# Gated attention: transposes ahead of sums in each matrix-engine slot, and sums emptied behind the low halves

## The reference, cut to what matters

```python
qn = layernorm(x, ln_q_g, ln_q_b)
q = qn @ Wq * scale
k, v = jnp.split(media @ Wkv, 2, axis=-1)      # 16 heads of 64
sim = jnp.einsum('bhid,bhjd->bhij', q, k)
sim = jnp.where(media_mask[:, None, None, :], sim, neg_inf)
attn = jax.nn.softmax(sim, axis=-1)
out = jnp.einsum('bhij,bhjd->bhid', attn, v)
x = x + jnp.tanh(attn_gate) * (out.reshape(...) @ Wo)
h = layernorm(x, ln_ff_g, ln_ff_b)
x = x + jnp.tanh(ff_gate) * (jax.nn.gelu(h @ W1, approximate=False) @ W2)
```

## Time and profile before

| | us |
|---|---|
| median of 3 runs | 2543.61 |
| lowest and highest run | 2537.76 and 2545.34 |
| profiled execution | 2532.09 |
| its span | 2530.3 |

### The profile page before, as it was taken

One profiled execution on the slowest core, in us unless ns is written; L12 is line 12 of the kernel. 1 busy time (PEld: TensorE's weight loads), 2 busy tenths in 40 slices (PEclk: granted clock), 3 DMA queues, 4 the chain that ended last, 5 costly groups with the idle time before them and its releaser, 6 DMA issues.

```text
span 2530.3 us, 40523 instructions
## 1 busy us (share of the span) xinstructions
PE 2384.6 (94%) x15802; PEld 1893.7 (75%) x15802; DVE 1542.7 (61%) x4193; ACT 1259.6 (50%) x2132; POOL 583.9 (23%) x666
## 2 busy tenths in 40 slices
PE   7778999999999999789999999899999999999998
PEld 4646999999999765456666666455799999999975
DVE  3247777777777426566666666312777777777730
ACT  2135555555555223267777777211555555555521
POOL 0014344444342004200000000000434444434200
PEclk9889999999999999899999999999999999999999
DMA  8710111112110200010000000310011111211010
GB/s 276 207 43 19 44 40 56 44 41 56 41 44 13 85 19 1 13 37 26 25 26 26 25 14 1 119 34 1 19 43 40 56 44 41 56 40 44 13 51 15
DMA packets 36092, 116.18 MB, mean 46 GB/s; under 512 B 4598, under 2 KB 18526, under 8 KB 35534
## 3 DMA queue, kind: packets, MB, share of 16 engines
q1 hardware_dynamic: 33438, 101.30, 13.3%
q10 hardware_dynamic: 2464, 12.29, 1.9%
HBM read 112.66 MB, written 0.92 MB: 45 GB/s over the span
## 4 chain that ended last, share of the span: by engine, by line
PE 85%; DVE 9%; ACT 3%; DMA 1%; issue 1%; POOL 0%; ACTq 0%; SPq 0%; DVEq 0%; POOLq 0%
PE bank L868 19%; PE bank L855 17%; PE bank L880 11%; DVE n_scores L1631 5%; PE bank L1512 4%; PE bank L1499 4%; PE bank L1524 3%; PE bank L1740 3%; PE bank L1090 2%; PE bank L1073 2%; PE bank L691 2%; PE bank L1081 2%; PE bank L1750 2%; PE bank L512 2%; PE bank L1485 1%; PE bank L368 1%
## 5 line engine op out<-in xcount | busy, mean ns | idle before, releaser
L929 ACT CAST p_T_high<-bank 125x512 fp32r<-125x512 f32 x672 | 350.9, 595 | 515.5 <-PE bank L880 515.5
L1002 DVE TENSOR_TENSOR p_T_low<-bank,p_T_high 125x512 fp32r<-125x512 f32 x672 | 422.7, 685 | 258.2 <-ACT p_T_high L929 258.0
L968 DVE CUSTOM_DVE_ANT_0 scores<-bank,mask 128x500 f32<-128x500 f32 x672 | 418.2, 672 | 0.4 <-PE bank L855 0.4
L939 ACT ACTIVATE scores<-scores,row_max 128x1500 f32<-128x1500 f32 x224 | 353.5, 1578 | 9.8 <-DVE row_max L973 9.8
L868 PE MATMUL bank<-p_T_high,keys_nat_high 125*128 125x256 f32 (+1 forms) x1152 | 346.2, 301 | 1.7 <-ACT inverse L936 1.7
L868 PE MATMUL bank<-p_T_high,keys_nat_low 125*128 125x256 f32 (+1 forms) x1152 | 346.1, 300 | 0.0
L868 PE MATMUL bank<-p_T_low,keys_nat_high 125*128 125x256 f32 (+1 forms) x1152 | 345.9, 300 | 0.0
L880 PE MATMUL bank<-ident,scores 128*125 128x128 f32 x2688 | 332.0, 273 | 2.4 <-ACT scores L939 2.4
L880 PEld LDWEIGHTS bank<-ident,scores 128*125 128x125 f32 x2688 | 319.4, 188 | 5.7 <-ACT scores L939 5.7
L1631 DVE CUSTOM_DVE_ANT_0 n_scores<-bank,n_zeros 112x500 f32<-112x500 f32 x384 | 237.5, 675 | 126.9 <-PE bank L1499 126.9
L855 PE MATMUL bank<-keys_T_high,q_stage_high 128*128 128x500 f32 x672 | 281.1, 418 | 10.5 <-DVE q_stage_low L945 6.9
(11 more groups left out here) (197 smaller groups left out, 3234.0 us busy)
## 6 DMA issues: line engine op xcount, KB each, us to landing
ctx_T<-in_ctxT SPq DMA_DIRECT2D x32, 750.0 KB, 4.3
ctx_nat<-in_ctx SPq DMA_DIRECT2D x32, 672.0 KB
q_and_o<-in_ctxT SPq DMA_DIRECT2D x16, 750.0 KB, 9.8
n_ctx_T<-in_ctxT SPq DMA_DIRECT2D x16, 750.0 KB, 4.3
q_and_o<-in_ctx ACTq DMA_DIRECT2D x16, 672.0 KB
mask_bytes<-in_mask SPq DMA_DIRECT2D x32, 187.5 KB, 5.3
weights<-in_L_W SPq DMA_DIRECT2D x4, 1024.0 KB, 9.6
ctx_nat<-in_ctx SPq DMA_DIRECT2D x32, 78.0 KB
```

Source lines behind the costliest of these rows:

```text
L929: e.copy(PTs[0][g % 2][0:KP, 4 * c:4 * c + 4, lo:lo + 128], psum[3 + c][0:KP, :].rearrange("p (k r) -> p k r", k=4)).then_inc(s_eh, 1)
L939: e.activation(SB[s % 2], SB[s % 2], ACT.Exp, bias=mx[:, s % 4, 3:4], accum_out=mx[:, s % 4, 4:5]).then_inc(s_ex, 1)
L968: e.tensor_tensor_reduce(out=SB[u % 2][:, c * CHK:(c + 1) * CHK], in0=psum[c][:, 0:CHK], in1=mb[:, c * CHK:(c + 1) * CHK], scale=1.0, scal ...
L1002: e.tensor_tensor(low, psum[3 + c][0:KP, :].rearrange("p (k r) -> p k r", k=4), high.bitcast(F32), ALU.subtract).then_inc(s_el, 1)
```

## The change

In PE's slot the transposes and the spread of unit s-1 move ahead of the sums; the slot is scores, transposes, spread, sums. In DVE's slot o_out moves behind the three low copies. No instruction is added or removed, and every wait keeps its place ahead of its instruction.

```diff
@@ pe_cross
             for s in range(U + 4):
                 if s < U:
                     scores(s)
-                for g, part, of in work_of(s):
-                    sums(g, part, of)
                 if 1 <= s <= U:
                     transposes(s - 1)
                     if units_of(group_of(s - 1))[-1] == s - 1:
                         spread(group_of(s - 1))
+                for g, part, of in work_of(s):
+                    sums(g, part, of)
@@ dve_cross
                     e.reciprocal(mx[:, u % 4, 5:6], mx[:, u % 4, 4:5]).then_inc(s_rc, 1)
-                for g, part, of in work_of(s):
-                    if part == of - 1:
-                        o_out(g)
                 if 0 <= u < U:
                     g = group_of(u)
                     lo = column(u)
...
                         e.tensor_tensor(low, psum[3 + c][0:KP, :].rearrange("p (k r) -> p k r", k=4),
                                         high.bitcast(F32), ALU.subtract).then_inc(s_el, 1)
+                for g, part, of in work_of(s):
+                    if part == of - 1:
+                        o_out(g)
```

## The result

| | before | after |
|---|---|---|
| median of the runs, us | 2544.48 (4 runs) | 2641.41 (4 runs) |
| lowest and highest, us | 2537.76 and 2546.4 | 2640.32 and 2647.06 |
| profiled execution, us | 2532.09 | 2640.32 |
| its span, us | 2530.3 | 2638.5 |
| ratio, 95% interval | | 1.039 (1.0366 to 1.0415) |

The change makes the kernel 3.9% slower, 96.9 us between the medians. 2647 us was forecast. The ratios of all runs leave out the one disturbed execution, 4013 us among the ten of the kernel with DVE's order alone.

A forecast was written before the change was run, and what follows sets the result against it. PE's instruction stream was taken as the bound. Stalls of 52 us in each gated-attention stage, 104 in both, less 0.5 at their ends, added 103.5 to 2543.6 us: 2647 us, 4.1% slower, range 2610 to 2685.

The forecast's parts named there:

- The bound: Gated-attention stages: PE's own instruction stream bounds them, with almost no idle time a new order could win back.
- The new wait and its slots: In slots 3 and 5 of seven, ACT's high copy waits for sums now behind the transposes, 31 times a stage.
- The size of the conflict stall: PE's transposes wait for Exp behind ACT's waiting copy: 1.23 us plus 0.11 for load, 1.34 us each.
- The load ahead: Twelve transposes that waited for Exp take 1.58 us against 1.47, their weights not loaded ahead: 0.11 us more.
- The second stall: Slot 4's spread waits for DVE's late reciprocal after slot 3's stall: 0.7 us with load, 15 times a stage.
- The sum: Both stages: 41.5 and 10.5 us make 52 in each, 104 in both; less 0.5 at the ends, 103.5 us.
- The prediction's own 0.5: Net gain at starts and ends of stages: 0.83 us of idle covered at the end, about 0.4 lost at the start.
- The 75 us: Changed profile: transposes wait for Exp about 31 times in each stage, near 1.2 us each, 75 us in all.
- The first rival's break point: Not slower, 5 in 100: the copy's delay stays under slack if less than some 0.9 us of sums follow the transposes.
- the slack of 1.62 us: From first copy to next slot's first transpose, 4.77 us, against a copy, Exp and read-out chain of 3.15 us.
- Clock and seams: Within the larger-wait rival, over 2672 us, 10 in 100: seams cost 18 us more, a 0.94 clock up to 80.

The follow-up runs named there:

- both repairs: Changed kernel with ACT's Exp ahead of the three high copies in slots 3 and 5 of seven, and DVE's reciprocal ahead of the maxima: 2543.4 us, ratio 1.0007.

## Why the prediction was right, and where it wasn't

- **The bound** (PE without gaps, nothing to win back): right. The two kernels of these runs that have no new wait in their repeating slots, DVE's order alone and the one with both repairs, give 1.0014 and 1.0007.
- **The new wait and its slots**: right. ACT waited for the sums 62 times, in slots 3 and 5 of seven, and Exp behind it in ACT's queue was shown to be the cause by taking it out of that queue.
- **The size of the conflict stall**: 1.23 us and 0.11 for the load were forecast. The same two distances in the kernel with both repairs give what a slot takes without a stall, 5.46 and 5.50 in the rows shown, so that 6.77 and 6.80 hold stalls of 1.31 and 1.30. The load is 0.11 as forecast (5.59 from 668.57 to 674.16, against 5.48 there, from 683.69 to 689.17). The copy started 3.63 us behind its transposes instead of 3.54, since the first sums matmul now carries the exposed load (it starts 0.26 us ahead of the second, the others 0.17 to 0.19), which the sum had placed at the scores. So 1.42 and not 1.34 us: 62 times 0.08 is some 5 us too little.
- **The load ahead**: the waiting blocks took 1.57 and 1.58 us, the others 1.47, as forecast. The Trainium skill ("TensorE: Matmul & The Clock Gate", Part 2, step 1) has weight loads pulled ahead of matmuls in flight. The rows don't contradict it, as the prediction had it: in the blocks that waited no matmul was left in flight, and there the 0.11 us stands.
- **The second stall**: the mechanism was right (two edits removed it, one enlarged it), the size too large. 0.7 us was forecast. The distance is 6.28 us, against 5.82 in the two kernels that have the conflict stall but not this one: 0.46. The reciprocal ended almost where it was reckoned, 10.70 us behind the start of slot 3's scores instead of 10.75, but only the second transpose of the spread needs it: the first turned unit 2's reciprocal ahead of time (656.90), and no further load shows. 30 times 0.24 is 7 us too much.
- **The sum**: 104 us less 0.5 was forecast, 100.5 lie in the stages, and the medians differ by 96.9. Two mis-sized terms of opposite sign, 5 us and 7 us, nearly cancel, and that is luck. With the measured sizes, 62 times 1.42 and 30 times 0.46, the sum is 102 us, and the starts and ends of the stages with the seams gave back 1 net. (The prediction's own 0.5 for them is a slip: 0.83 gained and 0.4 lost in each of two stages make 0.9.) The remaining 3.6 us between stages and medians is less than the 5.6 us by which an untouched stretch differed. The 75 us that the prediction wanted to see as PE's wait for Exp came out as 74.8 by luck too: 62 stalls are shown with 1.14 us each, some 71 us, and ten short waits at the starts and ends of the stages make up the rest.
- **The first rival's break point**: wrong, though the rival did not come true. "Less than about 0.9 us of sums left behind the transposes" set the sums' end against a fixed place of the next transposes, but that place moves with the sums. With 0.5 to 0.7 us left, the ratio was still 1.0396. The step that failed is the slack of 1.62 us: it was counted from a copy that does not wait.
- **Clock and seams**: neither took part. PE's granted clock stayed at 1.00 in both stages. PE was busy 639 of 685 us in the first, a larger share than the 626 of 682 that was forecast, since busy time grew with the waits, as estimated behind the page above:

```profile
200.00:885.00 685.00, 639.11 (x4158) 578.19 (x4159) 472.86 (x1289) 370.08 (x620) 251.70 (x290) 1.00 0.13 37
1830.00:2520.00 690.00, 643.76 (x4172) 580.21 (x4171) 474.91 (x1291) 371.81 (x623) 251.74 (x290) 1.00 0.13 36
```

## What to carry to other kernels

Before moving a producer within an in-order slot, ask which buffers its end sets free, who waits for them, and what is queued behind that waiter: here a wait that had always been over by the time it was asked held back an Exp which had nothing to do with the buffer. Measure a stall as the chain from what releases it to the next use against the work that lies between them; how much of the block was moved can cancel out. And after a repair look for what was late next: taking the Exp out of the queue gave back 37 us, and the remaining 61 needed the reciprocal too, which by itself had given back some 10.

## What the runs showed of the hardware that I had not expected

Nothing in kind. Two sizes are worth having: a block of twelve transposes that had to wait for Exp took 0.10 to 0.11 us more (1.57 or 1.58 against 1.47 us) in every kernel whose rows show such a wait, and the first start of such a block stands 0.05 us behind the end of Exp's accumulator read (655.49 against 655.44). And the stretch ahead of the first stage, which no edit touched, took 205.8 us in the profile before, 211.5 in the profile after, and up to 220.2 in those of the experiments, so that single profiles of 2.5 ms tell differences of a few us only if they are read stage by stage.
